# Routing weights by ScalarE in place of VectorE, with a new order table, in a two-layer transformer kernel

## What is computed

```python
gate_logits = jnp.einsum('ble,en->bln', x, gate_kernel)
top_k_weights, top_k_indices = jax.lax.top_k(gate_logits, TOP_K)      # TOP_K = 2
softmax_probs = jax.nn.softmax(top_k_weights, axis=-1)
weights = jnp.zeros_like(gate_logits).at[b_idx, l_idx, top_k_indices].set(softmax_probs)
layer_mult = jax.nn.silu(layer_w0) * layer_w1                         # for every expert
intermediate = jnp.einsum('blnh,nhe->blne', layer_mult, wo_kernel)
output = jnp.einsum('blne,bln->ble', intermediate, weights)
```

## Time and profile before

| | us |
|---|---|
| median of three runs | 965.92 |
| lowest and highest | 959.76, 969.08 |
| the profiled execution, as timed | 969.92 |
| its span, first to last instruction | 967.7 |

### The profile page before, as it was taken

One profiled execution on the slowest core, in us unless ns is written; L12 is line 12 of the kernel. 1 busy time (PEld: TensorE's weight loads), 2 busy tenths in 40 slices (PEclk: granted clock), 3 DMA queues, 4 the chain that ended last, 5 costly groups with the idle time before them and its releaser, 6 DMA issues. The chain is left out here.

```text
span 967.7 us, 15545 instructions
## 1 busy us (share of the span) xinstructions
PE 803.7 (83%) x4976; PEld 442.4 (46%) x4976; DVE 707.5 (73%) x1415; ACT 576.3 (60%) x907; POOL 469.6 (49%) x609
## 2 busy tenths in 40 slices
PE   4366776899889888999989999988998898688676
PEld 2111122345345534654455545654664466365354
DVE  6688578779878778867778888767686736567664
ACT  2245574757677667765777587567755854433332
POOL 4143125203567546782767376457557653862201
PEclk9669699899999999999899999999999999799787
DMA  6435044353655342295245355552337053110000
GB/s 179 147 106 132 33 81 156 105 116 104 219 139 148 118 137 72 75 273 152 67 110 179 122 156 126 173 172 76 89 102 232 15 176 123 58 38 20 1 23 27
DMA packets 101306, 110.65 MB, mean 114 GB/s; under 512 B 16409, under 2 KB 81049, under 8 KB 99882
## 3 DMA queue, kind: packets, MB, share of 16 engines
q1 hardware_dynamic: 97082, 102.06, 37.3%
q0 software_dynamic: 3584, 7.35, 2.3%
q10 hardware_dynamic: 560, 0.26, 0.1%
HBM read 82.98 MB, written 26.26 MB: 113 GB/s over the span
## 5 line engine op out<-in xcount | busy, mean ns | idle before, releaser
L1754 DVE TENSOR_REDUCE negmax<-scores_for_max 128x2 f32<-128x1024 f32 x252 | 307.6, 1221 | 80.8 <-PE scores_for_max L1050 73.7
L1453 ACT ACTIVATE probs<-scores 128x1024 f32<-128x1024 f32 x256 | 261.7, 1022 | 107.4 <-PE scores L1074 93.5
L1084 PE MATMUL weighted_values<-probs,vaug 128*32 128x512 f32 x1024 | 142.9, 636 | 0.0
L1050 PE MATMUL scores_for_max<-ks,qs 48*128 48x512 bf16 x504 | 103.3, 406 | 42.0 <-DVE negmax L1754 37.0
L1146 PE MATMUL expert_units<-xt,ring 128*128 128x128 f32 x840 | 119.8, 284 | 9.3 <-DVE mu L1938 6.1
L1146 PEld LDWEIGHTS expert_units<-xt,ring 128*128 128x128 f32 x840 | 103.2, 191 | 45.4 <-issue 44.6
L1074 PE MATMUL scores<-qs,ks 51*128 51x512 bf16 x512 | 104.3, 404 | 16.8 <-ACT probs L1453 14.6
L1050 PEld LDWEIGHTS scores_for_max<-ks,qs 48*128 48x128 bf16 x504 | 24.7, 94 | 126.8 <-DVE negmax L1754 96.7
L2217 POOL DMA_INDIRECT xs_d<-xbn,rowpos x56 | 55.0, 983 | 45.0 <-DVE rowpos L1887 30.1
L2228 POOL DMA_INDIRECT y<-ys_d,rowpos x56 | 55.4, 989 | 29.8 <-issue 15.7
L1199 PE MATMUL shared_ab<-ring,mu 128*128 128x128 f32 x420 | 57.8, 283 | 2.5 <-ACT slot_rows L1579 1.1
(11 more groups left out here) (329 smaller groups left out, 1572.0 us busy)
## 6 DMA issues: line engine op xcount, KB each, us to landing
ring<-in_experts SPq DMA_DIRECT2D x113, 384.0 KB, 5.0
slot_rows<-xs_d SPq DMA_DIRECT2D x7, 960.0 KB
parts_d<-parts SPq DMA_DIRECT2D x15, 384.0 KB, 2.7
qs<-parts_d SPq DMA_DIRECT2D x14, 384.0 KB, 6.2
ks<-parts_d SPq DMA_DIRECT2D x14, 384.0 KB, 9.7
ys_d<-slot_rows SPq DMA_DIRECT2D x21, 256.0 KB
w<-in_L_ffn_w SPq DMA_DIRECT2D x16, 256.0 KB, 4.1
parts_d<-parts SPq DMA_DIRECT2D x15, 256.0 KB, 2.9
```

Source lines behind the costliest of these rows:

```text
L1050: last = nc.tensor.matmul(max_bank(b, g, n)[:, 512 * m:512 * (m + 1)], qs[at, b % 2, p, t * P:(t + 1) * P], ks[at, b % 2, p, :], start=Tru ...
L1084: last = nc.tensor.matmul(pv[32 * j:32 * j + 32, :], vaug[:, kt, PAIRS * (j // 2) + GP * g + j % 2, :], probs[:, kt % 2, j % 2, j // 2, :] ...
L1453: nc.scalar.activation(probs[:, kt % 2, j, :, :].rearrange("p m s -> p (m s)"), se[:, :], ACT.Exp)\
L1754: V.tensor_reduce(negmax[:, g % 2, :, n], max_bank(b, g, n)[:, :].rearrange("p (m s) -> p m s", m=2), AX, ALU.max, negate=True)\
```

## The change

ScalarE makes the weights: t = tanh(difference / 2), then 1/4 - t/4 and 1/4 + t/4, which are the same two halves. VectorE keeps no step of it, except `place` in the last batch. A tile `quarter` holds the bias 1/4, and is one memset more among the first (SS_END from 5 to 6).

```diff
 def route(b):
     after(act, "b_pick", b, PICK_DIF)
-    nc.scalar.activation(pw[:, 1, :, :], pw[:, 0, :, :], ACT.Exp).then_inc(sig["b_e2"], 1)
+    if b == 0:
+        act.wait_ge(s_set, SS_END)
+    nc.scalar.activation(pw[:, 1, :, :], pw[:, 0, :, :], ACT.Tanh, scale=0.5).then_inc(sig["b_e2"], 1)
+    after(act, "b_e2", b, 1)
+    after(act, "b_t", b - 1, 2)
+    for c, sign_of in ((0, -1.0), (1, 1.0)):
+        nc.scalar.activation(pw[:, 2 + c, :, :], pw[:, 1, :, :], ACT.Identity, bias=quarter[:, :],
+                             scale=0.25 * sign_of).then_inc(sig["b_pw"], 1)
...
 def do_top(b):
...
-    after(dve, "b_pw", b - 1, 3)
+    after(dve, "b_e2", b - 1, 1)
     link_p(V.tensor_tensor(pw[:, 0, :, :], top[:, :, 1:2], top[:, :, 0:1], ALU.subtract))
...
 def do_weights(b):
-    after(dve, "b_e2", b, 1)
-    after(dve, "b_t", b - 1, 2)
-    V.tensor_scalar(pw[:, 2, :, :], pw[:, 1, :, :], 1.0, 2.0, ALU.add, ALU.mult).then_inc(sig["b_pw"], 1)
-    after(dve, "b_pw", b, 1)
-    V.reciprocal(pw[:, 3, :, :], pw[:, 2, :, :]).then_inc(sig["b_pw"], 1)
-    after(dve, "b_pw", b, 2)
-    V.tensor_tensor(pw[:, 4, :, :], pw[:, 3, :, :], pw[:, 1, :, :], ALU.mult).then_inc(sig["b_pw"], 1)
     if b == LAST:
-        after(dve, "b_pw", b, 3)
+        after(dve, "b_pw", b, 2)
         for c in range(2):
-            V.tensor_tensor(mine[:, c, :, :], pick[:, c, :, :], pw[:, 3 + c, :, :].to_broadcast([P, NT, NEX]),
+            V.tensor_tensor(mine[:, c, :, :], pick[:, c, :, :], pw[:, 2 + c, :, :].to_broadcast([P, NT, NEX]),
                             ALU.mult).then_inc(sig["b_place"], 1)
```

More of the change, by code:

```diff
@@ L87 @@
 SLOTS = {
[L88 to L93, removed]
@@ L303 @@
-        327, 328, 329)),
-        ("B", "x2"): dict(pool=(108, 144, 184, 228, 261, 299, 331, 332)),
-        ("C", "rstd"): dict(pool=(109, 146, 187, 231, 262, 301, 333, 346)),
-        ("C", "rstd2"): dict(pool=(112, 148, 192, 234, 265, 304, 336, 348)),
-        ("C", "lo"): dict(pool=(116, 154, 195, 237, 267, 306, 338, 340)),
-        ("C", "rstd3"): dict(pool=(129, 170, 213, 257, 298, 312, 347, 352)),
-        ("P", "rope"): dict(sp=(1, 13, 29, 30, 31, 32, 33, 34)),
-        ("P", "second"): dict(sp=(2, 4, 7, 8, 9, 10, 11, 12)),
@@ L311 @@
-        ("P", "raw"): dict(sp=(3, 20, 21, 22, 23, 24, 25, 26)),
-        ("P", "late"): dict(sp=(5, 35, 36, 37, 38, 39, 40, 41)),
-        ("B", "blank"): dict(sp=(6, 15, 16, 17, 18, 19, 27, 28)),
-        ("P", "load"): dict(sp=(14, 43, 58, 72, 84, 103, 124, 147)),
-        ("P", "store"): dict(sp=(42, 44, 62, 64, 67, 69, 79, 81, 98, 100, 119, 130, 142, 146, 164, 168)),
-        ("P", "modst"): dict(sp=(45, 46, 47, 48, 49, 50, 51, 52)),
-        ("P", "stack"): dict(sp=(53, 65, 71, 83, 101, 133, 148, 170)),
@@ L325 @@
[L325 to L328 removed]
+        ("C", "upb"): dict(pe=(1, 2, 3, 7, 16, 17, 18, 20, 21, 22, 25, 26, 27, 28, 1372, 1373)),
+        ("C", "out0"): dict(pe=(4, 5, 8, 19, 23, 24, 57, 1362)),
@@ new lines @@
+        ("B", "ldown"): dict(pe=(6, 9, 10, 11, 12, 13, 14, 15, 29, 30, 31, 32, 33, 34, 35, 36, 37, 38, 39, 40, 41, 42,
+        43, 44, 45, 46, 47, 48, 49, 50, 51, 52, 61, 62, 63, 64, 65, 66, 67, 68, 69, 70, 71, 72, 73, 74, 75, 76, 77,
+        78, 79, 80, 81, 82, 83, 84, 1313, 1317, 1321, 1323, 1333, 1335, 1338, 1340)),
+        ("C", "row"): dict(pe=(53, 54, 55, 56, 58, 59, 60, 1345)),
+        ("P", "wT"): dict(pe=(85, 86, 87, 88, 89, 90, 91, 92)),
+        ("P", "colm"): dict(pe=(93, 94, 96, 97, 98, 99, 100, 101, 102, 103, 109, 110, 111, 112, 113, 114)),
@@ new lines @@
+        1302, 1305, 1309, 1316, 1320, 1326, 1332, 1337), dve=(376, 383, 389, 395, 414, 423, 430, 437, 455, 461, 467,
[3 rows of a table added]
+        ("B", "downm"): dict(pe=(381, 382, 385, 386, 394, 396, 397, 401, 434, 435, 436, 437, 454, 455, 456, 528, 529,
[6 rows of a table added]
+        ("C", "xT"): dict(pe=(533, 681, 829, 992, 1099, 1246, 1322, 1353)),
+        ("C", "qk"): dict(pe=(538, 554, 693, 706, 833, 858, 997, 1028, 1114, 1137, 1257, 1263, 1324, 1334, 1360,
+        1361)),
+        ("C", "hid"): dict(pe=(567, 573, 582, 587, 718, 723, 739, 747, 872, 878, 892, 898, 1042, 1052, 1056, 1060,
@@ new lines @@
+        1150, 1156, 1171, 1177, 1273, 1275, 1300, 1303, 1339, 1346, 1347, 1348, 1355, 1356, 1358, 1359), act=(258,
+        261, 265, 268, 343, 346, 353, 356, 429, 432, 438, 441, 523, 528, 532, 535, 583, 586, 593, 596, 658, 659, 668,
+        670, 696, 698, 699, 700, 708, 710, 711, 712)),
+        ("C", "sim"): dict(pe=(596, 597, 598, 599, 730, 731, 732, 733, 883, 884, 885, 886, 1045, 1046, 1047, 1048,
+        1162, 1163, 1164, 1165, 1294, 1295, 1296, 1297, 1341, 1342, 1343, 1344, 1364, 1365, 1366, 1369)),
@@ new lines @@
+        ("C", "out"): dict(pe=(619, 620, 756, 757, 905, 906, 1065, 1066, 1184, 1185, 1306, 1307, 1349, 1350, 1374,
+        1375)),
+        ("C", "xT3"): dict(pe=(633, 779, 918, 1075, 1208, 1310, 1351, 1376)),
+        ("C", "up"): dict(pe=(635, 640, 648, 654, 783, 788, 800, 822, 924, 929, 939, 947, 1086, 1091, 1104, 1107,
+        1216, 1221, 1235, 1241, 1311, 1312, 1314, 1318, 1352, 1354, 1357, 1363, 1377, 1378, 1379, 1380), act=(292,
+        299, 306, 312, 378, 385, 397, 404, 454, 458, 466, 475, 552, 557, 562, 566, 620, 628, 637, 641, 675, 678, 683,
@@ new lines @@
+        ("B", "weights"): dict(dve=(7, 24, 25, 26, 27, 29, 30, 907)),
+        ("C", "qkgb"): dict(dve=(10, 14, 38, 39, 40, 42, 43, 44, 45, 46, 47, 48, 49, 50, 970, 971), pool=(118, 122,
+        160, 163, 197, 202, 244, 248, 269, 272, 307, 309, 341, 343, 344, 345)),
+        ("C", "keep3"): dict(dve=(15, 16, 17, 18, 19, 20, 21, 982), pool=(144, 186, 210, 261, 301, 330, 349, 350)),
+        ("B", "lacc"): dict(dve=(41, 51, 52, 53, 54, 55, 56, 57, 58, 59, 60, 61, 62, 63, 64, 65, 66, 67, 68, 69, 70,
@@ new lines @@
+        71, 72, 73, 74, 75, 76, 77, 78, 79, 80, 81, 82, 83, 84, 85, 86, 87, 88, 89, 90, 91, 92, 93, 94, 95, 96, 97,
+        98, 99, 100, 101, 102, 103, 104, 105, 913, 919, 924, 926, 938, 940, 943, 945)),
+        ("C", "keep"): dict(dve=(106, 107, 108, 115, 116, 117, 118, 958), pool=(116, 153, 194, 230, 265, 305, 337,
+        338)),
+        ("P", "stats"): dict(dve=(120, 201, 286, 342, 400, 463, 563, 693)),
+        ("P", "wsplit"): dict(dve=(122, 147, 148, 149, 166, 167, 168, 169)),
+        ("P", "cols"): dict(dve=(138, 141, 152, 153, 154, 155, 156, 157, 158, 159, 160, 161, 162, 163, 164, 165)),
@@ new lines @@
+        ("P", "whlo"): dict(dve=(140, 142, 143, 144, 145, 146, 150, 151)),
+        ("P", "lo"): dict(dve=(177, 178, 179, 180, 181, 182, 183, 184), pool=(20, 33, 41, 58, 81, 115, 169, 225)),
+        ("P", "rot"): dict(dve=(185, 186, 187, 191, 192, 193, 273, 282, 284, 288, 290, 292, 296, 298, 300, 305, 307,
+        309, 353, 355, 357, 361, 365, 367, 413, 417, 418, 428, 431, 439, 483, 486, 487, 518, 520, 521, 603, 604, 606,
+        609, 610, 611, 725, 726, 727, 730, 731, 732)),
+        ("P", "mod1"): dict(dve=(189, 196, 197, 199, 232, 233, 234, 235, 236, 237, 238, 239, 240, 241, 242, 243, 244,
@@ new lines @@
+        245, 246, 247, 248, 249, 250, 251, 252, 253, 254, 255, 256, 257, 258, 259)),
+        ("P", "split3"): dict(dve=(194, 200, 204, 205, 220, 221, 222, 223, 224, 225, 226, 227, 228, 229, 230, 231),
+        pool=(10, 11, 39, 44, 47, 52, 70, 74, 84, 97, 123, 149, 183, 190, 232, 247)),
+        ("A", "wog"): dict(dve=(272, 344, 408, 474, 556, 642, 734, 800)),
+        ("A", "onorm"): dict(dve=(303, 316, 325, 334, 351, 363, 379, 392, 409, 433, 444, 457, 485, 502, 516, 532, 568,
+        588, 601, 617, 655, 670, 689, 705, 747, 761, 769, 788, 841, 855, 872, 883)),
@@ new lines @@
+        ("B", "x1"): dict(dve=(337, 402, 465, 545, 631, 718, 794, 888)),
+        ("B", "stats"): dict(dve=(339, 404, 468, 548, 641, 719, 795, 889)),
+        ("B", "logits"): dict(dve=(346, 416, 497, 560, 652, 738, 812, 896)),
+        ("B", "top"): dict(dve=(347, 419, 498, 561, 653, 739, 816, 897)),
+        ("B", "place"): dict(dve=(349, 425, 500, 566, 656, 743, 819, 821)),
+        ("C", "stats"): dict(dve=(460, 539, 626, 712, 775, 854, 908, 946)),
+        ("C", "stats2"): dict(dve=(470, 550, 637, 722, 783, 862, 915, 956)),
@@ new lines @@
+        ("C", "stats3"): dict(dve=(524, 600, 687, 774, 848, 905, 953, 980)),
+        ("C", "upa"): dict(dve=(531, 538, 543, 551, 616, 624, 638, 643, 695, 699, 706, 713, 787, 796, 801, 805, 864,
+        868, 870, 873, 906, 910, 916, 921, 959, 961, 969, 973, 983, 984, 986, 989)),
+        ("C", "fin"): dict(dve=(559, 565, 654, 658, 735, 737, 817, 820, 875, 877, 931, 932, 975, 977, 991, 992)),
+        ("P", "slots"): dict(pool=(1, 4, 7, 8, 9, 13, 14, 21)),
+        ("B", "fold"): dict(pool=(12, 15, 16, 17, 18, 19, 22, 23, 24, 25, 26, 27, 28, 29, 311, 312)),
@@ new lines @@
+        ("P", "rstd"): dict(pool=(30, 32, 38, 57, 78, 110, 156, 220)),
+        ("A", "vcopy"): dict(pool=(31, 54, 76, 104, 141, 180, 222, 264)),
+        ("C", "w2g"): dict(pool=(34, 167, 207, 249, 297, 308, 342, 351)),
```

(41 more changed lines are left out.)

236 lines of the change are left out of this document (80 added, 156 removed), and 124 rows, old and new, of the table SLOTS.

## The result

The kernel after takes 973.62 us in the median of 12 runs (969.66 to 980.60); twelve runs of the kernel before beside it gave 966.69 (959.76 to 973.11). The ratio is 1.0075 [1.0049, 1.0101]: 0.75% slower, where the forecast was 0.4% faster. It lies within 1% and inside the range of 950 to 976, with the wrong sign. A second job gave 1.0105 [1.0070, 1.0141].

The account below looks back on a forecast made before the run. TensorE was taken as the bound from 200 to 800 us, with only 54.4 us of idle to win. Terms -3 + 0 + 4 + 0 - 5 = -4 gave 965.9 profiled, 962 us as median, 0.4% faster; range 950 to 976.

Parts of the forecast that it names:

- VectorE's removed work, -3: Weights' three VectorE instructions per batch: 12.9 us of busy time leaves, a quarter reaches the end, -3 us (0 to -12.9).
- ScalarE's added work, 0: Two more ScalarE steps per batch, 3.3 us in eight, hidden in ScalarE's idle: 0 us, bounds -4.5 and +3.3.
- behind its input: ScalarE's weights step: the new table puts it 40 and more places later, ending the old 4.5 us wait in three batches.
- Start, +4: Start-up order: later first store, `stack(0)` near 43 and first maximum near 50 cost +4 us, bounds 0 and 6.
- Middle, 0 with 8 either way: Batches 1 to 6: same work interleaved differently, taken as 0, with 8 us either way from TensorE's 54.4 us idle.
- End, -5: After 800 us: last expert 19 us earlier, 14 given back by batch 6's tail behind it; -5 us, bounds -12 and +7.
- rival 2: End stays idle, costing +7: 974 us; slower if the last expert comes forward by less than 15 us. Chance 0.18.
- Profile to median, -4: Whole kernel: 965.9 us from the profiled 969.9, then 962 because the kernel before's median lay 4.0 below its profiled run.
- What would show me wrong: Signs of error: start unchanged, middle alone moving over 8 us, or the new ScalarE chain making the last `weights` wait.

Follow-up runs that it names:

- the move alone: Kernel after with the kernel before's order table and two weight sets: 0.9975 of the kernel before where that takes 967 us, 0.9981 where 1006 to 1011.
- the one with the old end: Kernel after with the kernel before's order from batch 5's third transposes on: 1.0100 of the kernel before at 967 us, 0.9988 and 1.0018 at 1006 to 1011.
- the new middle: Kernel after with two weight sets and the kernel before's order at start and end: 1.0051 of the kernel before at 967 us, 0.9895 at 1006 to 1011.
- the old start: Kernel after with the kernel before's order up to batch 1's second maxima: 1.0066 of the kernel before at 967 us, 0.9885 at 1006 to 1011.

## Why the prediction was wrong, step by step

- **VectorE's removed work, -3.** Right. Busy time fell by 9.6 us with the move alone (12.9 forecast); the last exponential of batch 7 ended 4.1 us earlier in its trace (783.7 against 787.8), and the ratio says -2.4 [-5.4, +0.6]. A quarter reached the end by these figures, but the interval also holds nothing and half of it.
- **ScalarE's added work, 0.** Right in size, wrong in one sentence. Each Identity took 290 ns, not the 205 of the nearest row (the Copy and Exp had no bias held in a tile). By the Trainium skill (ScalarE: Activation LUTs, Rules for kernel authors) about 0.3 us was to be budgeted, and here the trace agrees with the page rather than with my row; at 4.6 us in all it was still hidden. But "behind its input" looked at one wait alone (and the step moved back by 30 to 55 places in batches 1 to 5 only, by 14 and 10 in the last two). It overlooked the second wait that the diff adds, for the old buffer: 4.8 us in the kernel after, 9.0 in the one with the old end.
- **Start, +4.** Right within what is known: +2.7 at the first `exp` of the trace, of which 1.0 is left when batch 0's exponentials end (127.6 us against 126.6), and 3.8 or 0.9 by the ratios. `stack(0)` at 42.65 (43 forecast), the first maximum at 49.31 (50.7), `w2g` without its wait.
- **Middle, 0 with 8 either way.** This is the step that failed: a new order was put at nothing. It was +7.3 on the faster chip: inside its bound, but the bound was drawn from TensorE's 54.4 us of idle, and the idle did not grow (163.9 us in the kernel before, 159.7 with the new middle). I used the granted clock only to tell stretches apart and gave it no term. The earlier trace rows had it in view: 0.85, 0.98, 0.89 in neighbouring stretches. A rearranged list changes where TensorE pauses, and the new end shows what that can do (0.98 to 0.87 from 850 to 903 us). That the same happens in the middle is argued from the clocks of the timed runs; no pause there is shown to bring it.
- **End, -5.** Failed in size. The last expert came 16.6 us forward (19 forecast). The give-back was 17.3 and not 14: 22.8 us between the last expert and the normalisation instead of 19.5, with `out` 1.4 us over its 2.0 and the last rounds 3.8 and 4.4 instead of 3.1, most of it half clock. Before it, batch 7's last exponential had ended 1.9 us ahead (785.9 against 787.8) and the product behind its attention (L1103, before L1101) began 0.1 ahead, so the end is worth +1 in the trace; the ratios give +1.5 together with the single buffer. My rival 2 puts this at "less than 15 us forward"; it came forward by more and the gain still went, so the rival's condition was wrong too. That its time of 974 is the median is luck: it put +7 at the end and nothing in the middle.
- **Profile to median, -4.** Failed. Against the profiled execution the sum of 965.9 missed 970.9 by 5.0, nearly all of it the end. The other 6.7 of the 11.6 us come from taking the kernel after to stand 4 below its profile as before did; it stood 2.8 above it (973.62 against 970.86).
- **What would show me wrong.** The list held: VectorE's time, the counts, `stack(0)`, `x2` of batch 6 (836.6 us; "near 833 plus what the start costs"), the last expert, bare rounds. All came out nearly as forecast and the time did not, because none of them was the clock.

What stays open: why the new middle is worse on the faster chip and better on the slower; which pause in it brings the clock down. The kernel with the new middle gains 15 us by the end of batch 3's attention and loses 21 of it by the end of batch 7's (milestones of its exponentials against the move alone: -15.0, then +6.2), so in this execution the loss lies nearly all in batches 5 to 7, where its clock falls at 503, 646, 663 and 687 us. The trace of the old start, with the same lists there, ends batch 7's attention 1.3 us ahead of the move alone. The two kernels differ up to there in the weight buffers alone, one set against two, and more runs would have to tell whether that or the scatter of executions is the reason. No kernel was run that changes from one order to the other inside the middle. Of the six kernels that ran on both chips, the move alone (0.9975 and 0.9981) is the only one below before on each, by less than can be told.

## What to carry to other kernels

When an edit reorders much of a TensorE-bound kernel, forecast the granted clock as a term of its own, with a range: busy time at each level, not just idle removed. Here 0.01 of mean clock went with 6 us of 967. Compare the clocks of many timed runs, not of two profiled ones, before trusting a difference of a few us. And where work moves to an engine that writes a single buffer, list the new write-after-read wait with what stands behind it.
